# Two transformer layers on one core: the bias rows of proj and fc2 as one 128-row product instead of two 33-row products

## The reference, cut to what matters

```python
# first layer
attn = softmax(mask(q @ k.T * D ** -0.5)) @ v              # per head
o = attn @ proj_w + proj_b                                 # proj: bias row 1
x = x + gate_msa * ((1 + scale_msa) * ln(o) + shift_msa)
h = gelu(x @ fc1_w + fc1_b)
m = h @ fc2_w + fc2_b                                      # fc2: bias row 2
x = x + gate_mlp * ((1 + scale_mlp) * ln(m) + shift_mlp)
# second layer
x = x + gate_s * (gelu(mod(ln(x)) @ ssm_w1 + ssm_b1) @ ssm_w2 + ssm_b2)
x = x + gate_f * (gelu_tanh(mod(ln(x)) @ ff_w1 + ff_b1) @ ff_w2 + ff_b2)
```

## Time and profile before

| what | us |
|---|---|
| median of 3 timed runs | 389.43 (389.39 to 389.55) |
| span of the profiled execution, first to last instruction | 386.9 |
| PE busy (2626 matmuls) | 355.4, 92% of the span |
| DVE busy | 250.7, 65% |
| ACT busy | 231.6, 60% |
| POOL busy | 177.0, 46% |

### The profile page before, as it was taken

The page is one execution under the profiler, slowest core; times in us unless marked ns, Lnnn a source line. Parts: engine busy times, 40 slices in busy tenths (PEclk is TensorE's granted clock), DMA queues, the critical chain, the costliest instruction groups (busy, mean ns, idle before and its releaser), DMA issues. The chain is left out here.

```text
span 386.9 us, 7689 instructions
## 1 busy us (share of the span) xinstructions
PE 355.4 (92%) x2626; PEld 288.2 (75%) x2626; DVE 250.7 (65%) x565; ACT 231.6 (60%) x440; POOL 177.0 (46%) x185
## 2 busy tenths in 40 slices
PE   6698699999999999999999999999998989997881
PEld 5586587455599967597897858879984889995671
DVE  5664736888983489988848597753456575348531
ACT  5521215778546588986687689787548836442630
POOL 1435249502526543252263633725655455564541
PEclk9889755999999999999999999999999999999998
DMA  6597981665543022300201010000000000000001
GB/s 235 190 327 246 279 264 61 193 173 177 158 151 118 3 65 62 97 9 31 71 0 44 4 42 3 2 28 29 3 0 2 0 30 29 2 2 0 0 8 57
DMA packets 20183, 30.90 MB, mean 80 GB/s; under 512 B 1934, under 2 KB 12808, under 8 KB 20137
## 3 DMA queue, kind: packets, MB, share of 16 engines
q1 hardware_dynamic: 16664, 23.24, 19.9%
q10 hardware_dynamic: 3472, 7.08, 5.5%
HBM read 21.20 MB, written 8.80 MB: 78 GB/s over the span
## 5 line engine op out<-in xcount | busy, mean ns | idle before, releaser
L604 POOL TENSOR_TENSOR p_hid<-p_gelu,p_hid 128x512 fp32r<-128x512 f32 x56 | 73.2, 1310 | 70.8 <-ACT p_hid L774 70.4
L879 DVE TENSOR_REDUCE p_nmax<-ps 128x2 f32<-128x512 f32 x128 | 82.4, 682 | 20.5 <-PE ps L1136 17.5
L743 ACT ACTIVATE p_probs<-ps 128x512 f32<-128x512 f32 x128 | 68.5, 602 | 15.9 <-PE ps L1148 14.0
L622 POOL TENSOR_TENSOR x_all<-x_all,p_vec 128x512 f32<-128x512 f32 x32 | 41.1, 1296 | 44.6 <-DMA p_vec<-pmod_dram 20.6
L1008 PE MATMUL ps<-p_fc_hi,p_hid 128*128 128x256 f32 x256 | 52.8, 289 | 0.7 <-POOL p_hid L604 0.7
L765 ACT ACTIVATE p_gelu<-ps,p_column 128x256 f32<-128x256 f32 x64 | 26.8, 469 | 29.0 <-PE ps L1008 27.8
L1008 PEld LDWEIGHTS ps<-p_fc_hi,p_hid 128*128 128x128 f32 x256 | 41.5, 188 | 3.1 <-POOL p_hid L604 1.1
L1008 PE MATMUL ps<-p_m_hi,p_fc_hi 128*128 128x256 f32 x128 | 36.8, 287 | 0.1
L774 ACT ACTIVATE p_hid<-p_gelu 128x512 fp32r<-128x512 f32 x56 | 35.2, 632 | 2.0 <-PE ps L1008 0.5
L765 ACT ACTIVATE p_gelu<-ps,p_upb_mod 128x256 f32<-128x256 f32 x48 | 20.1, 471 | 26.7 <-PE ps L1008 26.6
L1008 PE MATMUL ps<-p_fc_lo,p_hid 128*128 128x256 f32 x128 | 36.0, 281 | 0.0
(11 more groups left out here) (198 smaller groups left out, 882.3 us busy)
## 6 DMA issues: line engine op xcount, KB each, us to landing
p_qa<-pq_dram SPq DMA_DIRECT2D x28, 192.0 KB, 4.1
pq_dram<-p_qk_buf SPq DMA_DIRECT2D x6, 512.0 KB, 3.1
p_vec<-pmod_dram SPq DMA_DIRECT2D x4, 512.0 KB, 3.8
out<-x_all SPq DMA_DIRECT2D x8, 256.0 KB, 2.2
p_probs<-in_L_cond_ada_w ACTq DMA_DIRECT2D x1, 1536.0 KB, 9.4
pq_dram<-p_qk_buf SPq DMA_DIRECT2D x6, 256.0 KB, 5.1
p_adb_raw<-in_L_cond_ada_w ACTq DMA_DIRECT2D x1, 1536.0 KB, 9.5
x_all<-in_x SPq DMA_DIRECT2D x3, 512.0 KB, 7.0
```

The costliest lines, as they stand in the source:

```text
L604: pool.tensor_tensor(hid[:, TOOK[of][0], 1, :], gelu_out[:, TOOK[("gelu",) + step[1:]][0], :], hid[:, TOOK[of][0], 0, :].bitcast(F32), ALU ...
L622: pool.tensor_tensor(tiles(m, h), tiles(m, h), vec[:, m // NCH, SHIFT[L], :].rearrange("p (o c) -> p o c", o=1).broadcast_to([P, 2, C]), A ...
L743: act.activation(probs[:, kt, 2 * p + e, :], ps[:, TOOK["s2", a, g, kt, p][e], :], ACT.Exp, scale=SCALE).then_inc(s_exp, 1)
L879: dve.tensor_reduce(nmax[:, u % 2, e, 0, at:at + 2], ps[:, TOOK["s1", a, g, j][e], :].rearrange("p (t n) -> p t n", t=2), axis=AX.X, op=AL ...
```

## The change

The tiles `ones` and `bias_hl` get 128 partitions in place of 33 (the new rows of `bias_hl` are zero, since the tile is cleared whole). At each of the 16 places the two matmuls of 33 rows by 256 columns become one matmul of 128 rows by 512 columns; its moving operand is the same 256 columns of `bias_hl` read twice by an access pattern with step zero, and it starts the accumulation of the whole bank.

```diff
-    bias_hl = sb("p_bias_hl", [33, 2, C], F32R)
-    ones = sb("p_ones", [33, P], F32R)
+    bias_hl = sb("p_bias_hl", [P, 2, C], F32R)
+    ones = sb("p_ones", [P, P], F32R)
...
+        def bias_rows(which):
+
+            return bias_hl[:, which:which + 1, :].broadcast_to([P, 2, C])
...
-                for t in range(2):
-                    pe.matmul(dst[:, t * C:(t + 1) * C], ones[0:33, :], bias_hl[:, 0, :], start=t == 0, stop=False, skip_group_check=True)
+                pe.matmul(dst.rearrange("p (t c) -> p t c", t=2), ones[:, :], bias_rows(0), start=True, stop=False, skip_group_check=True)
...
-                    for t in range(2):
-                        pe.matmul(dst[:, t * C:(t + 1) * C], ones[0:33, :], bias_hl[:, 1, :], start=t == 0, stop=False, skip_group_check=True)
+                    pe.matmul(dst.rearrange("p (t c) -> p t c", t=2), ones[:, :], bias_rows(1), start=True, stop=False, skip_group_check=True)
```

## The result

| | kernel before | changed kernel |
|---|---|---|
| median of 20 runs each, taken side by side | 389.62 us | 385.83 us |
| lowest and highest | 385.87, 402.42 us | 379.18, 499.39 us |
| ratio by the comparison, 95% interval | | 0.9838 [0.9807, 0.9870] |
| profiled execution, and its span | time not given, 386.9 us | 386.08 us, 384.4 us |

The kernel is faster. By the medians it gains 3.8 us, and 385.83 is what was forecast. The ratio takes of each kernel only the runs within 1.5% of its own fastest; with one run at 379.18 that leaves 8 of the 20 of the changed kernel, against 17 of the 20 of before, and so it leans to the changed kernel's side. By the means of all runs but 402.42 and 499.39 (389.32 and 385.19) the gain is 4.1 us.

The account below looks back on a forecast made before the run. PE was taken to bound the kernel from 100 to 285 us. Gains of 3.12 + 0.28 + 0.18 = 3.58, so 3.6 us off the median 389.43, gave 385.8 us, range 383.9 to 387.2.

Parts of the forecast that it names:

- What bounds the kernel: From 100 to 285 us PE sets the pace; time taken out of its queue comes off the end.
- 0.86 to 0.47 at a place: PE, last product ahead of a bias to second behind: 0.86 us before, 0.47 with 128 rows; each place frees 0.39.
- Which places keep it: Of 16 bias places, eight keep all 0.39 us (3.12), two keep part, the others nothing, by PE's next wait.
- the six of the forecast's "nothing": Bias places proj/0/0, dn/fc/1/1, dn/fc/2/1, dn/fc/3/1, proj/3/1 and proj/3/0, each forecast to add nothing to the sum.
- The two parts: Two places keeping part of the gain: proj/2/1 with 0.28 us and dn/fc/2/0 with 0.18 us.
- A sign of being wrong that appeared: PE's waits from 100 to 285 us growing to more than 1 us in sum would mean fewer places keep gain.
- The sum: Gain over all bias places: 3.12 + 0.28 + 0.18 = 3.58, so 3.6 us off.
- Rivals 1 and 2: At the bias: first, extra belongs to the ones step, 388.4 us, chance 0.06; second, columns alone count, 389.4 us, 0.05.
- rival 1: Extra belongs to the step between activations and ones, not to rows; 1.0 us saved, 388.4 us; chance 0.06.
- Rival 3: TensorE's clock falls to 1.2 GHz in the tail, chain's products take up to twice as long, 395.7 us; chance 0.04.
- Rival 4: More bias places keep their gain, up to 384.0 us (chance 0.08), or fewer do, down to 387.4 us (0.09).
- The 2.5 us around the span: Median 389.43 minus profiled span 386.9, taken as time around the span that stays unchanged.

## Why the forecast was right, and where it was not

- *What bounds the kernel.* Right: from 100 to 285 us PE set the pace, and what left its queue left the middle stretch.
- *0.86 to 0.47 at a place.* Right in size, at every place in 128-row surroundings with no wait close behind. Its four extras of 0.1 were rightly sized, but one was misplaced: it stands behind the first product of few rows, not at the border between two of them, so one 33-row product in place of two saved none of the 0.10 that the sum's lower bound gave it.
- *Which places keep it.* Right: eight forecast to keep 3.12 kept 2.84 + 0.44 = 3.28 in the changed kernel and 3.1 to 3.2 by themselves; the six of the forecast's "nothing" kept -0.06 together. The two parts were 0.18 and 0.32 for 0.28 and 0.18: behind proj/2/1 the 0.28 came and 0.10 of it was lost again on the way out of s2; at dn/fc/2/0 PE took POOL's low part 0.01 behind its end (261.24 + 1.34 = 262.58, then 262.59), not 0.15, which frees 0.22, and another 0.10 came in small steps up to the next place.
- *A sign of being wrong that appeared.* PE's waits from 100 to 285 us sum to 1.1 us, over the 1 us that was to mean fewer places. It misled: the window cut off a wait of 0.37 of the kernel before at 285.35, and no fewer places kept their gain.
- *The sum.* 3.58 was forecast; the middle stretch is 3.4 to 3.7 shorter in five traces, the mean of 47 runs 3.74 below that of 117.
- *Rivals.* Rivals 1 and 2 are ruled out by the 0.47, and rival 1 once more by the two 128-row products. Rival 3 did not occur. Rival 4: neither more nor fewer places.
- *The step that failed* is the error given to the sum. The range, 383.9 to 387.2, had terms for the places and the rivals and none for the stretches that the change doesn't touch: the time ahead of the first place ("ahead of 100 us no bias product stands") and behind the last product was taken as one fixed number, and a measurement was to tell "0.2%, 0.8 us, from no change"; three runs within 0.2 us seemed to allow it. Over twelve executions these stretches measure 97.0 to 104.3 us ahead of the first place and 7.0 to 9.0 behind the last product, and the kernel before against itself came out at 1.000 with +-0.0047 (1.8 us). So a ratio from 8 of 20 runs could give 383.1, below the range, though the gain was sized rightly: with a spread of about 2.5 us, 8 runs leave some 0.9 us by chance alone (2.5 / square root of 8), and the way in which the 8 are chosen adds to it on one side.
- *Luck.* That the median of 20 runs, 385.83, meets the forecast to 0.03 us is luck: by the same spread it is known to no better than about half a us (2.5 / square root of 20), and the places gave 3.72 in this trace where 3.58 was summed.
- *The 2.5 us around the span* are not around it. In every run that lists both, the time is 1.6 to 1.8 us longer than the span; by that the profiled execution of before took about 388.6 us (an estimate, 386.9 + 1.7) and was 0.8 us shorter than the median. The forecast was a difference from the median and did not change by it, but it was a first trace of the spread.

Not settled: why the stretch at the low clock is longer in some executions, and why the last output takes longer to land in some. No run here was made for either.

## To carry to other kernels

A matrix product of at most 64 rows that stands alone among products of 128 cost some 0.4 us more here, 0.2 on the way in and 0.2 on the way out, whether one of 512 columns or two of 256. Where the rows can be filled with zeros, fill them beyond 64; where they can't, such products cost less in a row than one at a time among others. Ask place by place which wait ends last behind it: the freed time of a full engine was kept or lost nearly whole at 13 of 16 places, and taking still more out of the same queue paid a quarter. And before a change of under 1% is judged by a ratio, cut several traces at the first and last instruction that the change can move: here the piece between was steady within 0.2 us for kernels of the same gain while whole runs of one kernel spread by 9.

## What was not expected

- The change between few rows and many is what costs: about 0.1 us ahead of the first product of the new kind and 0.1 behind it, in either direction, at the 2.4 GHz level. The border lies between 64 and 65 rows, with nothing between. The Trainium skill, page "TensorEngine Tiling (Array Packing)", section "Tiling Modes", has the array split into two halves of 64 rows and says that a change of mode drains it. The border between 64 and 65 rows agrees with the halves, and the extra agrees with a price for the change of mode, 0.2 us each time; that it is a drain no run here shows. What the rows do show is that a product which follows a pause of PE has the same extra behind it: 282.20 - 281.97 = 0.23 behind a wait of 0.53, where 0.12 is usual.
- Two such products in different halves run beside each other: in s1, two products of 49 rows and 256 columns start 3 ns apart, and in the middle of a run the next pair follows 0.12 us later, the time of one 128-row product. This was not tried on the bias, whose two halves share a bank of PSUM.
- The same kernel spent 30.8 and 37.6 us at the low clock ahead of 104 us in two executions, and 27.3 to 41.0 over twelve executions of the two kernels and their variants.
